# Attention output of a fused macaron block taken back from memory in the layout it was written in

## What is computed

```python
x = x + 0.5 * ffn(layernorm(x))        # base 512x512 plus top-2 of 8 LoRA experts of rank 16
x = x + attn(layernorm(x))             # q, k, v, o by sign(W) times a scale per output column
x = x + 0.5 * ffn(layernorm(x))

scores = einsum('bhqd,bhkd->bhqk', q, k) / sqrt(16)     # 32 heads of 16, 8 key/value heads
out = einsum('bhqk,bhkd->bhqd', softmax(scores), v)
return bitnet_linear(out.transpose(0, 2, 1, 3).reshape(b, s, 512), o_weight, o_scale)
```

## Time and profile before

| | us |
|---|---|
| median of three runs (lowest, highest) | 1158.16 (1157.06, 1159.91) |
| profiled execution | 1159.3 |
| its span | 1157.5 |
| PE busy in the span | 1076.3 (93%) |
| DVE busy | 844.4 (73%) |
| ACT busy | 727.1 (63%) |
| GpSimd (POOL) busy | 293.3 (25%) |

### The profile page before, as it was taken

One profiled execution on the slowest core, in us unless ns is written; L12 is line 12 of the kernel. 1 busy time (PEld: TensorE's weight loads), 2 busy tenths in 40 slices (PEclk: granted clock), 3 DMA queues, 4 the chain that ended last, 5 costly groups with the idle time before them and its releaser, 6 DMA issues.

```text
span 1157.5 us, 16340 instructions
## 1 busy us (share of the span) xinstructions
PE 1076.3 (93%) x5968; PEld 484.5 (42%) x5968; DVE 844.4 (73%) x1146; ACT 727.1 (63%) x1361; POOL 293.3 (25%) x485
## 2 busy tenths in 40 slices
PE   5989887999999999999999999999999999998857
PEld 3778661344334433344334333433343334333436
DVE  5766679767776778877888678777977887782173
ACT  6457432757865787675776567666766675768420
POOL 5365556302510250410140014003200320041010
PEclk9989886999999999999999999999999999999979
DMA  7122331021210113011210121031002001300300
GB/s 254 38 90 88 101 103 49 28 65 26 61 34 32 30 53 83 27 32 38 68 27 26 53 54 26 26 81 27 26 26 80 27 27 26 81 6 7 90 1 36
DMA packets 87359, 59.42 MB, mean 51 GB/s; under 512 B 44144, under 2 KB 73328, under 8 KB 87280
## 3 DMA queue, kind: packets, MB, share of 16 engines
q1 hardware_dynamic: 87280, 58.39, 17.6%
HBM read 37.64 MB, written 20.32 MB: 50 GB/s over the span
## 4 chain that ended last, share of the span: by engine, by line
PE 74%; DVE 12%; ACT 6%; POOL 3%; issue 3%; DMA 1%; SPq 1%; DVEq 0%; POOLq 0%
PE ps_out L1452 20%; PE ps_score L1440 18%; PE ps_max L1415 16%; PE ps_fill L1373 5%; DVE neg_max L1218 3%; ACT probs L954 3%; PE ps_fill L1400 2%; PE ps_fill L1341 1%; PE ps_fill L1355 1%; PE ps_fill L1377 1%; DVE neg_max L1043 1%; DVE zd L1110 1%; PE ps_out L1373 1%; PE ps_max L1429 1%; PE ps_fill L1347 1%
## 5 line engine op out<-in xcount | busy, mean ns | idle before, releaser
L954 ACT ACTIVATE probs<-ps_score 128x512 f32<-128x512 f32 x992 | 539.0, 597 | 272.5 <-PE ps_score L1440 270.8
L1218 DVE TENSOR_REDUCE neg_max<-ps_max 128x1 f32<-128x1024 f32 x480 | 572.1, 1220 | 168.6 <-PE ps_max L1415 167.0
L1415 PE MATMUL ps_max<-kst,qst 96*128 96x512 bf16 x1024 | 294.0, 388 | 14.6 <-DVE neg_max L1043 5.7
L1440 PE MATMUL ps_score<-qst,kst 99*128 99x512 bf16 x992 | 305.1, 385 | 1.2 <-ACT probs L954 0.8
L1452 PE MATMUL ps_out<-probs,v_ring 128*32 128x512 f32 x2048 | 273.6, 606 | 8.1 <-ACT o_sb L960 5.3
L1440 PEld LDWEIGHTS ps_score<-qst,kst 99*128 99x128 bf16 x992 | 77.8, 97 | 254.3 <-ACT probs L954 210.0
L1415 PEld LDWEIGHTS ps_max<-kst,qst 96*128 96x128 bf16 x1024 | 88.4, 98 | 143.3 <-issue 17.6
L793 POOL CAST shift<-neg_max 128x16 bf16<-128x16 f32 x32 | 7.5, 236 | 463.3 <-DVE neg_max L1218 458.9
L1452 PEld LDWEIGHTS ps_out<-probs,v_ring 128*32 128x32 f32 x2048 | 41.0, 108 | 101.9 <-issue 92.0
L889 ACT ACTIVATE xn<-xc,ln_shift,rstd 128x512 f32<-128x512 f32 x48 | 38.5, 811 | 30.0 <-POOL ln_shift L690 19.0
L1373 PE MATMUL ps_fill<-wb_h,xt_h 128*128 128x512 f32 x84 | 46.9, 559 | 1.6 <-DVE xc L1205 0.8
(11 more groups left out here) (254 smaller groups left out, 1331.8 us busy)
## 6 DMA issues: line engine op xcount, KB each, us to landing
qst<-q_dram SPq DMA_DIRECT2D x192, 64.0 KB, 2.2
q_dram<-zm SPq DMA_DIRECT2D x24, 256.0 KB, 2.6
kst<-k_dram SPq DMA_DIRECT2D x192, 32.0 KB, 2.2
xc<-x SPq DMA_DIRECT2D x8, 512.0 KB, 3.8
x_dram<-xc SPq DMA_DIRECT2D x8, 512.0 KB, 2.8
xc<-x_dram SPq DMA_DIRECT2D x8, 512.0 KB, 4.2
out<-xc SPq DMA_DIRECT2D x8, 512.0 KB, 3.2
att_dram<-att SPq DMA_DIRECT2D x31, 128.0 KB, 2.2
```

Of the source, the lines that this page charges most:

```text
L954: act.activation(probs[:, kt % 2, j, :], score_bank(i, uu, j), ACT.Exp, scale=1.0 / HD ** 0.5).then_inc(probs_ready, 1)
L1218: dve.tensor_reduce(neg_max[:, uu % 2, t:t + 1], ps_max[max_slot(uu, pos)][:, :, :], AXY, ALU.max, negate=True).then_inc(max_read, 1)
L1415: last = pe.matmul(ps_max[slot][:, half, :], qst[0:SR, r, j, q * P:(q + 1) * P], kst[0:SR, r, half * 512:half * 512 + 512], start=True, st ...
L1440: pe.matmul(score_bank(i, uu, j), kst[0:SR + PARTS, uu, kt * P:(kt + 1) * P], qst[0:SR + PARTS, uu, j, :], start=True, stop=True).then_inc ...
```

## The change

The output stays in channels by tokens. SP stores `o_sb` itself (values and row sums, 256 KB a unit, at kt = 1). For a back chunk SP loads in slot 2 the row sums of all 32 heads as 128 rows of 64 (`sums`) and the values as four pieces of 128 channels by 256 tokens (`att_t`, the memory of `xn`). DVE inverts the sums in slot 4 (step NR), SP stores the reciprocals and loads them back with each row repeated 16 times (NL, `recip_t`, the memory of `zd`). The chunks of the bodies take the buffers of streams 0 and 1 in turn. Steps N0a and N0b multiply the two on DVE and round on ACT, N0al and N0bl make the low part. For the tail the loads stand in the last slots of body 7, and the last unit's values and sums are copied from `o_sb` by 16 DMAs after it (`load_last_out`); the sums are inverted there in the tail. One empty half slot after R5 is taken out, so that steps from Oa to R5 lie one half slot later and those from WR on where they were.

```diff
 BACK = [s.split() for s in (
-    12 * [""] + ["T0a", "T0al", "", "T0b", "T0bl", "", "Oa0", "Oa1", "C0", "Ob0", "Ob1", "", "G0 C1", "P0", "", "G1", "P1",
+    8 * [""] + ["NR", "NL", "", "", "", "", "", "N0a", "N0al N0b", "N0bl", "", "Oa0", "Oa1", "C0", "Ob0", "Ob1", "", "G0 C1", "P0", "", "G1", "P1",
     "ADD", "", "LN1a", "LN1b", "", "LN1c", "LN1d", "T1a", "T1al", "", "T1b", "T1bl", "", "RT", "", "RU",
-    "R0", "R1", "R2 HT0", "R3 R4 HT1", "R5", "", "", "WR", "", "WH FFa0", "WL FFa1", "FFa2", "FFa3 FFa4", "",
+    "R0", "R1", "R2 HT0", "R3 R4 HT1", "R5", "", "WR", "", "WH FFa0", "WL FFa1", "FFa2", "FFa3 FFa4", "",
     "FFb0", "FFb1", "FFb2", "FFb3 FFb4"])]
 
 F_USES = ["T1a", "T1b", "RT", "RU", "HT", "WR", "FFa", "FFb", "T2a", "T2b", "VK", "Q0", "Q1", "VT"]
-B_USES = ["T0a", "T0b", "Oa", "Ob", "T1a", "T1b", "RT", "RU", "HT", "WR", "FFa", "FFb"]
+B_USES = ["Oa", "Ob", "T1a", "T1b", "RT", "RU", "HT", "WR", "FFa", "FFb"]
...
-        self.load = (n + 1) * 16 if self.front else 16 * FRONT_PAIRS + n * 48 + (32 if tail else 48)
+        self.load = (n + 1) * 16 if self.front else 16 * (FRONT_PAIRS + n + 1)
+        self.att = slot if tail else n % 2
+        self.att_use = (n // 2 if slot == 0 else 3) if not self.front else 0
...
+        att_t = [t[:, :, :].rearrange("p t d -> p (t d)").rearrange("p (c n) -> p c n", c=DC) for t in xn]
+        recip_t = [t[:, 0:DC * CH].rearrange("p (c n) -> p c n", c=DC) for t in zd]
...
+                heads = att_dram[bass.ds(a // 2, 1), :, :, (a % 2) * CH:(a % 2) * CH + CH].rearrange(
+                    "o k (j x) t -> (o k j) x t", x=2 * HD)
+                known = H - REP if ch.tail else H
+                groups = P // H
+                sp.dma_start(sums[ch.att][0:known * groups, :],
+                             heads[0:known, HD, :].rearrange("h (g t) -> h g t", g=groups)).then_inc(sums_loaded[ch.att], 16)
+                for c in range(DC):
+                    h0, h1 = c * (P // HD), min((c + 1) * (P // HD), known)
+                    sp.dma_start(att_t[ch.att][0:(h1 - h0) * HD, c, :], heads[h0:h1, 0:HD, :]).then_inc(att_loaded[ch.att], 16)
...
+                sp.wait_ge(recip_ready[ch.att], ch.att_use + 1)
+                sp.dma_start(recip_dram[a, 0:known, :].rearrange("h (g t) -> h g t", g=groups),
+                             sums[ch.att][0:known * groups, :]).then_inc(recip_stored[ch.att], 16)
...
+                sp.wait_ge(recip_stored[ch.att], (ch.att_use + 1) * 16)
+                for c in range(DC):
+                    h0, h1 = c * (P // HD), min((c + 1) * (P // HD), known)
+                    sp.dma_start(recip_t[ch.att][0:(h1 - h0) * HD, c, :],
+                                 recip_dram[a, h0:h1, :].unsqueeze(1).broadcast_to([h1 - h0, HD, CH])
+                                 ).then_inc(recip_loaded[ch.att], 16)
...
+                sp.wait_ge(o_copied, NU)
+                for j in range(REP):
+                    to = slice(((KV - 1) % 2 * REP + j) * HD, ((KV - 1) % 2 * REP + j + 1) * HD)
+                    for dst, r0 in ((att_t[ch.att], 32 * j), (recip_t[ch.att], 32 * j + HD)):
+                        sp.dma_start(dst[to, DC - 1, :], o_sb[r0:r0 + HD, (NU - 1) % 2, s * CH:s * CH + CH]
+                                     ).then_inc(last_out_loaded[s], 16)
...
-            def store_att(i, uu, use):
+            def store_att(i, uu):
 
                 j = i + uu // UB
-                sp.wait_ge(max_read, use + 1)
-                sp.dma_start(att_dram[bass.ds((j // 2) * QT, QT), bass.ds((j % 2) * UB + uu % UB, 1), :, :]
-                             .rearrange("q o p d -> p q (o d)"), att[:, uu % 2, :, :]).then_inc(att_stored[uu % 2], 16)
+                sp.wait_ge(o_copied, i * UB + (uu + 1))
+                sp.dma_start(att_dram[bass.ds(j // 2, 1), bass.ds((j % 2) * UB + uu % UB, 1), :, :]
+                             .rearrange("o k p t -> (o k p) t"), o_sb[:, uu % 2, :]).then_inc(att_stored[uu % 2], 16)
...
-                    if kt == 4 and not (first and uu == 0):
-                        store_att(i, uu - 1, turn_use(i, uu, last))
-                    if slot == 5 and load_next is not None:
+                    if kt == 1 and not (first and uu == 0):
+                        store_att(i, uu - 1)
+                    if slot == 2 and load_next is not None:
+                        if load_next.n > 0:
+                            sp.wait_ge(filler_ready[0], Chunk("back", 0, load_next.n - 1).written("T1b"))
+                        load_att(load_next)
+                    if slot == 4 and load_next is not None:
                         load_x1(load_next, chunk_loaded[0])
-                        load_att(load_next)
-                    if last and slot == 8 * UB - 2:
+                    if last and slot == 8 * UB - 5:
                         sp.wait_ge(filler_ready[0], load_next.written("T1b"))
                         for ch in tail:
                             load_att(ch)
                         load_x1(tail[1], x1_loaded[1])
+                    if last and slot == 8 * UB - 3:
+                        for ch in tail:
+                            store_recip(ch)
+                    if last and slot == 8 * UB - 2:
+                        for ch in tail:
+                            load_recip(ch)
...
+            for ch in tail:
+                load_last_out(ch)
...
+                if pos in ("N0a", "N0b"):
+                    t = 0 if pos.endswith("a") else 1
+                    act.wait_ge(att_normed[s], n * 2 + (t + 1))
+                    act.activation(xt_h[s][:, :, t * P:(t + 1) * P], att_t[ch.att][:, :, t * P:(t + 1) * P],
+                                   ACT.Copy).then_inc(xt_h_ready[s], 1)
...
+                unit = UB * i + uu
+                if unit >= 2:
+                    act.wait_ge(att_stored[unit % 2], 16 * (unit // 2))
...
+                dve.wait_ge(sums_loaded[ch.att], (ch.att_use + 1) * 16)
+                dve.reciprocal(sums[ch.att][0:known * (P // H), :], sums[ch.att][0:known * (P // H), :]).then_inc(recip_ready[ch.att], 1)
...
+                if pos in ("N0a", "N0b"):
+                    t = 0 if pos == "N0a" else 1
+                    tok = slice(t * P, (t + 1) * P)
+                    dve.wait_ge(att_loaded[ch.att], (ch.att_use + 1) * 16 * DC)
+                    dve.wait_ge(recip_loaded[ch.att], (ch.att_use + 1) * 16 * DC)
+                    if ch.tail and t == 0:
+                        late = slice((KV - 1) % 2 * REP * HD, P)
+                        dve.wait_ge(last_out_loaded[s], 16 * 2 * REP)
+                        dve.reciprocal(recip_t[ch.att][late, DC - 1, :], recip_t[ch.att][late, DC - 1, :]).then_inc(last_recip_ready[ch.att], 1)
+                        dve.wait_ge(last_recip_ready[ch.att], 1)
+                    dve.tensor_tensor(att_t[ch.att][:, :, tok], att_t[ch.att][:, :, tok], recip_t[ch.att][:, :, tok],
+                                      ALU.mult).then_inc(att_normed[s], 1)
+                if pos in ("N0al", "N0bl"):
+                    t = 0 if pos == "N0al" else 1
+                    tok = slice(t * P, (t + 1) * P)
+                    dve.wait_ge(xt_h_ready[s], ch.t0 + (t + 1))
+                    dve.tensor_tensor(xt_l[s][:, :, tok], att_t[ch.att][:, :, tok], xt_h[s][:, :, tok].bitcast(F32),
+                                      ALU.subtract).then_inc(att_low_ready[s], 1)
...
-            def copy_rows(i, uu, use, slot, copied):
+            def copy_rows(i, uu, use, slot):
...
+                    if piece == 0:
+                        pe.wait_ge(att_low_ready[s], ch.n * 2 + (t + 1))
...
-            def turn(i, uu, use, slot, rows=True, out=True):
+            def turn(i, uu, use, slot):
 
                 max_slot_free(use)
-                if rows:
-                    pe.wait_ge(shift_parts, i * (4 * UB) + 4 * (uu + 2))
-                    last = pe.transpose(ps_max[slot][:, 0, 0:P // 2].bitcast(BF16), shift[:, (uu + 1) % 2, :], identb[:, :])
-                if out:
-                    pe.wait_ge(o_copied, i * UB + uu)
-                    for q in range(QT):
-                        last = pe.transpose(ps_max[slot][:, 1, q * P:(q + 1) * P], o_sb[:, (uu - 1) % 2, q * P:(q + 1) * P],
-                                            ident[:, :])
-                last.then_inc(max_scores, 1)
+                pe.wait_ge(shift_parts, i * (4 * UB) + 4 * (uu + 2))
+                pe.transpose(ps_max[slot][:, 0, 0:P // 2].bitcast(BF16), shift[:, (uu + 1) % 2, :],
+                             identb[:, :]).then_inc(max_scores, 1)
```

More of the change, by code:

```diff
@@ L1259, in body @@
                         if not (last and uu == 3):
[L1260 to L1262 removed]
+                            copy_rows(i, uu + 1, use, at)
+                    if last and slot == 8 * UB - 4:
+                        for ch in (Chunk("back", 0, 6, tail=True), Chunk("back", 1, 0, tail=True)):
+                            invert_sums(ch)
                     for pos, t in pairs[:1]:
@@ L1466, in body @@
```

(5 more changed lines are left out.)

97 lines of the change are left out of this document (44 added, 53 removed).

## The result

| | before | changed |
|---|---|---|
| median of 20 runs each, us | 1158.55 | 1162.52 |
| lowest, highest | 1155.65, 1161.78 | 1157.51, 1164.98 |
| profiled span, us | 1157.5 | 1161.0 |
| ratio, 95% interval | | 1.0030, 1.0018 to 1.0041 |

The changed kernel is slower by 0.3%, 4.0 us. Forecast was 1157.7, a hair faster than before; it came out slower. The result lies inside the stated range of 1149 to 1164, but outside the 1154 to 1161 of my own case. The spans differ by 3.5 us, so the two traces show nearly the whole loss.

A forecast was written before the change was run, and what follows sets the result against it. PE was taken to bound the bodies, with DVE and ACT right behind, and the engine-to-engine chain the tail. 1159.3 - 5.5 (bodies) + 5.0 (tail) = 1158.8, or 1157.7 us on the median's footing; range 1149 to 1164.

The forecast's parts named there:

- my own case: Whole kernel: bodies and end about cancel, 1157.7 us on the median's footing, within 1154 to 1161; chance 0.42.
- signs I had named: Wrong if a back body takes under 109.5 or over 113 us, or the end grows by under 2 or over 9.
- The turn: Row turns in the bodies: four transposes and DVE's reciprocal and multiply go, 0.67 us a turn, 11.6 us gained in sum.
- the zero for slot 17: Turn of slot 17 gains nothing, as LN1b stands ahead of the maxima's copy; bounds 0.3 gained, 0.2 lost.
- T0 and N0: Back bodies: eight transposes a chunk go, 5.3 us gained; new DVE multiplies in slots 8 and 9 cost 10.2 us.
- the replay of slots 8 and 9: Step-by-step timing of these slots with the new multiplies: 8.2 us against 6.5 without Oa, 1.7 us lost a body.
- NR, NL and the loads: Back bodies: DVE's reciprocal of 64 columns costs 0.2 us a body, 1.2 in all; DMAs cost nothing while covered.
- a cover of 2.6 us: Slot 5 store and four loads of the reciprocals land about 2.6 us before N0a asks for them.
- late in every body: Rival: output loads over 4.8 us make reciprocals late; at 6 us, 1.2 us a body, 1165 us; chance 0.09.
- The end: Tail after the last copy_out: first Oa 3.3 us later, then 1.7 us more; 5.0 us lost, bounds 2.5 and 9.
- the end is dearer: Rival: the 16 small copies issue at 0.59 each and land late, reciprocals take 2.2 us; 1161.5, 1162 or more; chance 0.16.
- the slower cases: Outcomes slower than before: dearer end, reciprocals late in every body, and causes not seen; chance given as 0.25.

The follow-up runs named there:

- experiment 3: Changed kernel with x1's load behind the reciprocals, SP also waiting for slot 6's third or slot 7's first score before storing them: 1178.3 and 1185.2 us.

## Why the prediction was wrong

The forecast said that bodies and end about cancel, with a slight gain; the bodies gave 3.3 us where 5.5 were forecast, the end took 5.9 and the start 0.9, and the kernel became slower. One of the signs I had named showed itself in the profile: body 2 took over 113 us. By its own steps, with the profiled spans:

- **The turn**: 0.67 each; the seven of bodies 0 and 1 gave 3.9 us of 4.0. Slot 25 gave 0.65 (bodies 2 to 6). Right, the zero for slot 17 too.
- **T0 and N0**: the replay of slots 8 and 9 was right in its chain, and 0.3 us too dear: 7.87 against 8.2. A body is 110.7 where 111.1 was forecast. That is 0.8 us to the good in bodies 4 to 6 and 0.6 in body 7.
- **NR, NL and the loads: the step that failed.** "The DMAs cost nothing as long as their cover holds", with a cover of 2.6 us. It was put together from medians of DMAs that stood alone: a landing of 2.2 for the store, issues of 0.46, another landing. Behind x1's load the store took up to 4.6, the issues 0.62 each, and from the first load issue to the release of N0a 5.9 us passed and not 4.0. From the store to the place where DVE reaches N0a there are 9.3 us. The forecast's 6.2 fits into them, 4.6 + 5.9 does not; either error alone would still have fitted, which is why putting x1 behind was enough. The 5.9 does not come from x1 standing ahead: with x1 issued behind the loads (experiment 3) it was 5.3 to 6.7. Where N0a came in time, the loads had begun 5.5 to 7.7 us ahead of it (bodies 4 to 7), so the slack there was small; in bodies 2 and 3 there was none. Instead of 0.6 us gained they lost 2.9: 3.5 of the 4.0 us by which my sum missed the span. The rival "late in every body" had the place and the mechanism, but it laid the lateness on the loads of the output and not on the store, and had only the lateness as its price; with what was lost behind the waits, 1.6 us of waiting became 4.1.
- **The end**: 5.9 of 5.0. Mis-sized were the copies' issue (0.62 and not 0.46) and the reciprocal (1.75 and not 1.5), together 1.4 on the first Oa, which came at 10.6 us after the end of `copy_out` where 8.9 was forecast. From the first Oa to A's G0 another 2.3 us was lost (11.1 us against 8.8), 1.7 by forecast, and 1.3 us came back behind `ADD`, which I had not counted. The rival "the end is dearer" named the 0.59 issue; its condition, landing 7.5 us after `copy_out`, was not met (6.6 in the prediction's count, 7.2 from the start of `copy_out`), and it was not what decided.
- **Not foreseen**: 0.9 us before the first turn, in which no instruction changed. It lies within what the profiles differ by there (4.2 us) and may be chance.
- **Slips in the prediction itself**, without weight for the result: "the end is dearer" takes its price from 5.0 where the sum has 5.3, and the slower cases add to 0.28 (0.16 + 0.09 + 0.03) and not 0.25.

3.5 (bodies 2 and 3) + 0.9 (end) + 0.9 (start) + 0.1 (front turns) - 1.4 (other bodies) = 4.0 us.

Of reciprocals, 128x64 took 543 ns and 64x256 1749: 6.3 ns a column between them, where 128x2 and 128x16 had given 5.2. The Trainium skill, "VectorE: DVE Perf Modes", section "First, the fixed hardware budget", would have given an estimated 2.1 us for the large one by its repeat count of 8: too much, as 5.2 was too little. The page's direction was right, the trace's row was the nearer. On the other rule, of the Trainium skill's "DMA: Bandwidth & Descriptors", section "Rules for kernel authors" (leading dimension below 16), no run here tells half the engines from all: the loads were late by their order, and in time once x1 stood behind them.
